# Loading each image in one transfer instead of two halves, in a kernel of dynamic convolutions

## The reference

```python
f = relu(einsum('oc,nchw->nohw', Wc, x) + bc)                 # 256 -> 64 channels
gk1 = relu(mean(x, axis=(2, 3)) @ Wc.T + bc)                  # from the channel means
g_kern = gk1[:, :, None] * Wkk + bkk
xm = x.reshape(N, C, k, H // k, k, W // k).max(axis=(3, 5))   # block maxima, k = 3
sk = relu(einsum('oc,nckl->nokl', Wc, xm) + bc)
dynW = relu(einsum('oj,ncjkl->nockl', Wck, stack([g_kern, sk])) + bck)
y = conv3x3(f, dynW)                                          # one set of weights per image
out = x + einsum('oc,nchw->nohw', Wf, y + b_ad) + bf          # 64 -> 256 channels
```

## Time and profile before

| | |
|---|---|
| median of 3 runs | 513.71 us |
| lowest to highest | 510.99 to 513.99 us |
| the profiled execution's own time | 512.45 us |
| its span, first to last instruction | 510.6 us |
| busy share PE, PEld, DVE, ACT, POOL | 95%, 75%, 82%, 84%, 58% |
| mean granted TensorE clock | 0.987 of full speed |
| moved by all transfers | 158.01 MB, 309 GB/s over the span |

### The profile page before, as it was taken

The page is one execution under the profiler, slowest core; times in us unless marked ns, Lnnn a source line. Parts: engine busy times, 40 slices in busy tenths (PEclk is TensorE's granted clock), DMA queues, the critical chain, the costliest instruction groups (busy, mean ns, idle before and its releaser), DMA issues.

```text
span 510.6 us, 19208 instructions
## 1 busy us (share of the span) xinstructions
PE 487.3 (95%) x8338; PEld 382.4 (75%) x8338; DVE 418.9 (82%) x653; ACT 426.5 (84%) x486; POOL 296.0 (58%) x231
## 2 busy tenths in 40 slices
PE   4897999999999999999999999999999999999993
PEld 2353765578787688888888877888888888888881
DVE  6779878978878988888889878888898888888544
ACT  5679899989979999999999989999999999995231
POOL 5233775455775555567755556776555567765543
PEclk9789999999999999999999999999999999999998
DMA  8935678999989999899999999999899999974467
GB/s 339 420 124 200 217 273 298 367 337 323 318 316 330 337 360 351 307 347 312 309 357 341 362 339 313 335 333 320 328 367 371 310 325 315 320 284 154 158 266 296
DMA packets 48868, 158.01 MB, mean 309 GB/s; under 512 B 4752, under 2 KB 15888, under 8 KB 48784
## 3 DMA queue, kind: packets, MB, share of 16 engines
q1 hardware_dynamic: 48784, 156.78, 85.6%
HBM read 75.94 MB, written 75.50 MB: 297 GB/s over the span
## 4 chain that ended last, share of the span: by engine, by line
PE 80%; ACT 2%; DVE 0%; issue 0%; DVEq 0%; ACTq 0%
PE ps L1120 30%; PE ps L1252 22%; PE ps L1220 21%; PE ps L1171 7%; ACT unused L610 1%; DVE X L850 0%; ACT unused L597 0%; ACT f_hi L689 0%; DVEq L153 0%; ACT f L695 0%; ACT Y L587 0%; ACT dyn_hi L708 0%; ACT dyn_b L710 0%; PE ps L1364 0%; ACTq L130 0%
## 5 line engine op out<-in xcount | busy, mean ns | idle before, releaser
L850 DVE SCALAR_TENSOR_TENSOR X<-ps,out_bias,X 128x960 f32<-128x960 f32 (+1 forms) x189 | 185.2, 1008 | 15.9 <-PE ps L1252 15.5
L1252 PE MATMUL ps<-Y,const 64*64 64x480 f32 (+1 forms) x1536 | 165.9, 486 | 0.0
L597 ACT ACTIVATE unused<-X,neg_mean 128x2304 bf16<-128x2304 f32 x60 | 132.0, 2201 | 0.4 <-DVE neg_mean L989 0.4
L513 POOL TENSOR_TENSOR dyn_a<-const,pool_g 128x576 f32<-128x576 f32 x30 | 35.0, 1165 | 166.3 <-DVE pool_g L874 166.3
L610 ACT ACTIVATE unused<-X 128x2304 bf16<-128x2304 f32 x60 | 126.9, 2114 | 0.0
L1220 PE MATMUL ps<-X,wcn_t 64*64 64x384 f32 (+1 forms) x1296 | 116.2, 486 | 1.2 <-issue 1.1
L926 DVE TENSOR_REDUCE feats<-X 128x6 f32<-128x1536 f32 x64 | 111.6, 1745 | 0.0
L1220 PEld LDWEIGHTS ps<-X,wcn_t 64*64 64x64 f32 x1296 | 83.7, 133 | 29.1 <-issue 6.7
L1252 PEld LDWEIGHTS ps<-Y,const 64*64 64x64 f32 x1536 | 79.4, 133 | 6.6 <-issue 2.0
L528 POOL TENSOR_TENSOR f_lo<-f,f_hi 128x1152 f16<-128x1152 f32 x32 | 71.5, 2233 | 21.7 <-ACT f L695 21.7
L1120 PE MATMUL ps<-f_hi,dyn_hi 64*64 64x480 f16 x1152 | 70.2, 369 | 4.2 <-ACT dyn_hi L716 2.8
(11 more groups left out here) (101 smaller groups left out, 539.2 us busy)
## 6 DMA issues: line engine op xcount, KB each, us to landing
X<-x SPq DMA_DIRECT2D x63, 1152.0 KB, 9.2
out<-X SPq DMA_DIRECT2D x61, 1152.0 KB, 8.4
out<-X SPq DMA_DIRECT2D x6, 480.0 KB, 3.5
stack<-f_hi SPq DMA_DIRECT2D x64, 32.5 KB, 2.4
stack<-f_lo SPq DMA_DIRECT2D x64, 32.5 KB, 5.7
X<-x SPq DMA_DIRECT2D x2, 576.0 KB, 7.1
upper<-f_hi SPq DMA_DIRECT2D x32, 32.5 KB, 3.7
out<-X SPq DMA_DIRECT2D x3, 192.0 KB, 3.0
```

What stands on the lines that cost most here:

```text
L597: nc.scalar.activation(unused[:, t], pixels(u, t), ACT.Square, scale=1.0 / SIDE, bias=neg_mean[:, n % 2, 1:2], accum_out=feats[:, (n + 1) ...
L850: nc.vector.scalar_tensor_tensor(out=out, in0=unit_psum(piece, bank, col), scalar=out_bias[:, t:t + 1], in1=out, op0=ALU.add, op1=ALU.add) ...
L1252: mm = nc.tensor.matmul(ps[rows, bank + q, col:col + width], wft[lanes, t, rows], Y[lanes, n % 2, at:at + width], start=True, stop=True)
```

## The change

Images 4 and up are loaded by one transfer of both halves, into the same places and pieces as before. It is issued where half 1 was: behind the stacks of f's high part. It waits for the stores of both halves of the image that used the place. It adds to `loaded[u][0]` only, and `wait_loaded` waits on that one for either half of such an image. Images 0 to 3 are loaded as before.

```diff
         def wait_loaded(eng, u, lap, t):
 
-            eng.wait_ge(loaded[u][t], (lap + 1) * 16)
+            n = u + RING * lap
+            eng.wait_ge(loaded[u][t if n < AHEAD else 0], (lap + 1) * 16)
...
+            def load_image(n):
+                u, lap = n % RING, n // RING
+                for t in range(HALVES):
+                    wait(sp, stored[u][t], lap, per=16)
+                whole = X[:, half(u, 0):half(u, HALVES)].rearrange("p (q f) -> p q f", q=2 * HALVES)[:, :, 0:HPIX]
+                sp.dma_start(whole, x[n].rearrange("(p t) f -> p (t f)", t=HALVES)
+                             .rearrange("p (q f) -> p q f", q=2 * HALVES)).then_inc(loaded[u][0], 16)
...
                     if inside(i - 2):
                         store(i - 2, 1)
-                    if i + AHEAD < N:
-                        load(i + AHEAD, 0)
                     stack_rows(f_hi, 0, i + 1)
                     if i + AHEAD < N:
-                        load(i + AHEAD, 1)
+                        load_image(i + AHEAD)
                     if inside(i - 1):
                         store(i - 1, 0)
                     stack_rows(f_lo, 1, i + 1)
```

## The result

The changed kernel takes 557.15 us (median of 6 runs), the kernel before beside it 513.09: a ratio of 1.0876, with a 95% interval of 1.0848 to 1.0904. It is slower by 8.8%, 44 us, where 522 us were forecast, with a range up to 538. The sign and the mechanism were right; the size was not. The profiled execution has a span of 555.8 us against 510.6.

The account below looks back on a forecast made before the run. TensorE, busy 95%, bounded the kernel; the load loop would replace its period. Turns +9.4, air -1.3, start +0.9 gave +9.0 on 512.45, 521.5, with about half the median's 1.3 us offset 522; range 511 to 538.

Parts of the forecast that it names:

- The loop: f_hi, stacks on SP, load, ScalarE's mean: turn 5.16 us plus landing time, forecast 15.11 us against TensorE's 14.61.
- L: Whole-image load's time from issue to landing behind the high-part stacks: taken as 9.95 us; over 9.45 the loop binds.
- rows 6: Landing times of loads back to back: 2.85 us apart, 414 GB/s, taken for the second half of the load.
- 24 turns: Loop turns counted from the load at 87.19 to that at 440.42: 353.2 us before, 362.6 forecast, +9.4 us.
- the 1.2 us over the half alone: Half load behind the stacks, 7.1 us against 5.9 alone; the excess was taken as slowness at the load's start.
- The upper bound of the prediction: Both halves of the load slow: landing 11.15 us, turn 16.31, 550 us; chance 0.08.
- the prediction's own sign of being wrong: In the changed profile, the whole-image load landing within 9.4 us, or taking 11 us or more.
- The start and the end: Waits for the loads of images 4 and 5 before the loop: +0.9 us; no separate cost for the last load.
- ScalarE's air: Slack before TensorE waits: 0.46 us before f_hi plus 0.84 before `dyn_hi`, 1.3 us, taken off once.
- The load was not hidden: Rival at ScalarE's L610: load lands within 9.45 us, only the start pays, 513 to 514 us; chance 0.24.
- The low-part stacks: Rival: behind a whole image they lose at most 2.85 of 7.8 us spare, still 514; chance within the hidden load's 0.24.
- nothing would become faster: Rival of fewer, larger transfers: TensorE waits for none, at most 1 us gained, 512; chance of over 1% faster 0.04.

Follow-up runs that it names:

- e1: Changed kernel with two half-image transfers behind the high-part stacks, each half's reader waiting for its own: 510.1 us, 0.9954 of the kernel before.
- e2: Changed kernel with the single whole-image transfer issued ahead of the high-part stacks: 510.1 us, 0.9951 of the kernel before.
- e5: Changed kernel with the whole-image load ahead of the three high-part stacks but behind the wait for f_hi: 513.83 us, ratio 1.002.
- e10: Changed kernel with two half transfers, readers waiting for both, and only 128 pixels per half stored for images 0 to 28: 524.96 us, ratio 1.0252.
- e4: Changed kernel with AHEAD = 5 instead of 4, each whole-image load issued one image earlier: 570.66 us, ratio 1.1142.

## Why the prediction was right and wrong

**The loop: right.** f_hi, stacks, load, mean, and round again, as e1, e2 and e5 show each from another side, and in the changed kernel as 5.16 + 11.1 = 16.3 of 16.39 us. The 0.1 us that is left lies between the stacks and the load. For 19 of the 25 loads from image 7 on that takes 1.83 to 1.86 us, but for six 2.16 to 2.96 (2.25 in the rows above, 238.03 to 240.28), because an issue on SP takes longer there; why isn't shown.

**L: the step that failed.** "I take 7.1 + 2.85 = 9.95 us: the slow part of a load is most likely its start ... and the second half then streams at the rate of rows 6." The term was 1.15 us too small (11.1 in the median), and 24 turns of it are 27.6 us of the 35 by which the forecast missed. Most of the rest is the start and the end, below.

Which part of the term was it? Not the start, and not the store behind the load: the 7.1 us of a half had a store behind it, issued 1.04 us later, so the 1.2 us over the half alone paid for that. It was the 2.85 us for the second half. Image 4 shows it without any large store. Its half 0 alone landed after 5.9 us, its single transfer in the changed kernel, issued at 41.74, after 10.1: 4.2 us for the second half. (Half 1 of that image, which stood in the same place as the single transfer, landed after 6.2, which leaves 3.9.) First the last stretches of the half, in the kernel before:

```profile
33.41:34.41 1.00, 1.00 (x10) 0.22 (x6) 0.96 (x1) 1.00 (x3) 0.00 (x0) 1.00 0.82 336
34.41:35.31 0.90, 0.90 (x12) 0.53 (x12) 0.59 (x2) 0.52 (x2) 0.00 (x0) 1.00 0.15 44
```

Then those of the whole image, in the changed kernel:

```profile
47.74:49.74 2.00, 2.00 (x16) 0.99 (x14) 2.00 (x3) 2.00 (x2) 0.00 (x0) 1.00 1.01 398
49.74:51.84 2.10, 2.10 (x16) 0.96 (x12) 2.06 (x5) 0.21 (x2) 1.36 (x2) 1.00 0.14 42
```

Nearly all bytes of the half had moved 5.0 us after issue, and of the whole image 8.0: these 3.0 us are about the 2.85 of rows 6, and so far the prediction was right. But then the half landed after 0.9 us more, and the whole image only after 2.1, in which the transfer engines were busy for 0.14 of the time. The landing has to wait for a last part, and in the single transfer this part comes late. The sum is 4.2 - 2.85 = 1.35 us too little for the second half, and 1.2 - (11.1 - 10.1) = 0.2 us too much for the neighbours: 1.15. Why the last part of the single transfer comes so late isn't shown. The rows of the prediction couldn't show it, since none had a transfer of this size. With two transfers and small stores (e10) the turn is 15.25 us, near the 15.11 forecast; so the forecast number fits another case than the one it was made for.

The upper bound of the prediction, 11.15 us, with a turn of 16.31 and 550 us, was the measured case. It held a chance of 0.08, and the range was drawn to leave it out. That its number fits is luck in part: the reason given for it (a slower rate in both halves) is not what the trace shows. But a bound next to which a row stood (7.4 us) deserved more, and the prediction's own sign of being wrong, 11 us or more, is what came.

**Another size for L.** The Trainium skill, *DMA: Bandwidth & Descriptors*, Anatomy of one DMA, fits 2.0 us plus bytes at 436 GB/s to a transfer issued from GpSimd. That is an estimate of 7.4 us for the image, and 11.1 were measured here behind the stacks, 12.0 in e2 and 10.1 with nothing large behind it. By that estimate the change would have been free. The measurement decides: for SP's transfers in this kernel the fit is too short.

**The start and the end: too small.** +0.9 us forecast for the start, 3.45 measured. Image 4's load landed after 10.1 us though no large store was behind it, and ScalarE waited for it and for image 5's:

```profile
51.88 2.12 ACT L617 ACTIVATE unused<-X 128x2304 bf16<-128x2304 f32 x1 [1.92 <-DMA X<-x]
...
67.72 2.12 ACT L617 ACTIVATE unused<-X 128x2304 bf16<-128x2304 f32 x1 [2.41 <-DMA X<-x]
```

And 24 turns were counted for 25 loads: the last load's own landing, 2.3 us more, was left out.

**ScalarE's air: wrong in place, too large in size.** The prediction had 1.3 us and TensorE waiting for Y behind `dyn_hi`. It waits for the full f (L702), behind which comes an output product in the same memory: f ends at 222.85, the product starts at 222.91. So the 0.84 us of idle time before `dyn_hi` were not the ones that counted. About 0.6 us came back at the end instead of 1.3; whether this is the whole reason isn't shown.

**The other rivals.** The load was not hidden: of the 21 between 100 and 440 us none landed within 9.45 us (10.1 at the least). The low-part stacks did land later (10.5 us in the median), and no wait of TensorE for them is among the changed kernel's waits: no cost, as said. That they can hurt, once SP issues them late enough, is shown by e4. That nothing would become faster was wrong for e1 and e2, by 0.5%, but these are not the change.

## What to carry to other kernels

Before two transfers become one, ask who waits for the first of them, and follow what it releases: if the next issue is among it, the landing of the whole transfer becomes a term of the period, at each image anew. Then size this landing by a transfer of the same form and size, with the same neighbours in the queue, and let the range reach to the slow bound when the period hangs on it at the rate of one to one. Here the same single transfer costs nothing when it is issued before the wait (e2, 510.1 us), and 8.8% behind it.

## What the runs showed of the hardware that was not expected

A load of 2.36 MB in one transfer, with nothing large behind it, had moved nearly all its bytes 8.0 us after issue and landed at 10.1. A load of half the size did so at 5.0 and 5.9. With a large store behind it in the queue the load lands 0.9 us later than with small ones (11.1 against 10.2 us), and between six and eight microseconds after issue 267 GB/s are moved instead of 372. One transfer of four pieces lands later than two of two pieces by channels, by 0.77 us a turn with large stores and 0.34 without; two by pixels and four of one piece lie between (15.87 and 15.88 us a turn). The causes of these are open. Leaving out the last quarter of a load brought its landing forward by 2.2 us, where its bytes at 414 GB/s are 1.4 us. Last, e1 and e2 beat the kernel before by 0.5%. Its turns were 14.72 us on average against 14.59 in e1, the same work; in the trace of before TensorE stood once for 1.1 us with nothing named as the cause, which e1's doesn't show. The 24 turns differ by 3 us, so this is a part at most, and the rest is open.
